# Expert stage of a graph network: blocks of two node tiles and an order for each engine

## What is computed

```
x = x + gnn0(layernorm(x), src, dst, edge_type, ...)   # relational sums over edges
x = x + ffn0(layernorm(x), ...)                        # router, 6 experts, top 2 of them
x = x + gnn1(layernorm(x), edge_attr, edge_weight, ...) # edge attention, then a feed-forward
x = x + ffn1(layernorm(x), ...)                        # router, 8 experts, top 2 of them
```

## Time and profile before

| what | value |
|---|---|
| median of three runs | 1781.44 us |
| the profiled execution, its own time | 1790.08 us |
| its span, first to last instruction | 1788.4 us |
| PE busy, share of the span | 1502.8 us, 84% |
| DVE, ACT, POOL busy | 1012.2, 585.6, 812.5 us |
| mean granted clock of PE | 0.885 |

### The profile page before, as it was taken

One profiled execution on the slowest core, in us unless ns is written; L12 is line 12 of the kernel. 1 busy time (PEld: TensorE's weight loads), 2 busy tenths in 40 slices (PEclk: granted clock), 3 DMA queues, 4 the chain that ended last, 5 costly groups with the idle time before them and its releaser, 6 DMA issues. The chain is left out here.

```text
span 1788.4 us, 22498 instructions
## 1 busy us (share of the span) xinstructions
PE 1502.8 (84%) x6333; PEld 951.4 (53%) x6333; DVE 1012.2 (57%) x2410; ACT 585.6 (33%) x1378; POOL 812.5 (45%) x769
## 2 busy tenths in 40 slices
PE   5999789469598898998736689998989899899996
PEld 3555235135254454456523356676766666676685
DVE  6532343133244453435358778887978787797432
ACT  3211012023132232323112145544445454444431
POOL 1100575757786677100067664745647374550000
PEclk9999659689799899999855689999999999999998
DMA  8356553645665655401188975656556565651100
GB/s 279 139 200 206 151 150 93 187 128 152 164 171 137 185 157 154 132 1 65 65 249 255 272 224 164 195 151 179 167 166 174 161 187 151 190 153 37 31 3 12
DMA packets 191806, 270.00 MB, mean 151 GB/s; under 512 B 28564, under 2 KB 156273, under 8 KB 189105
## 3 DMA queue, kind: packets, MB, share of 16 engines
q1 hardware_dynamic: 147665, 144.74, 26.1%
q0 software_dynamic: 44000, 123.64, 25.1%
HBM read 196.22 MB, written 72.06 MB: 150 GB/s over the span
## 5 line engine op out<-in xcount | busy, mean ns | idle before, releaser
L1853 POOL DMA_INDIRECT att_kv<-table_kv,g_srcI x314 | 366.1, 1166 | 301.2 <-issue 244.4
L1134 POOL DMA_INDIRECT ex_hg<-table_h,z_idx x314 | 322.9, 1028 | 114.6 <-issue 86.6
L1442 PE MATMUL ex_psG<-ex_hg,ex_oh 128*42 128x256 f32 x628 | 128.3, 467 | 91.8 <-issue 78.7
L2377 PE MATMUL att_psR<-att_t,g_mw 128*128 128x256 f32 (+1 forms) x640 | 163.0, 402 | 0.0
L2404 PE MATMUL att_psR<-g_mw,att_h 128*128 128x256 f32 x640 | 159.7, 395 | 1.0 <-ACT att_h L2222 1.0
L1845 POOL DMA_DIRECT2D table_o<-att_part x59 | 53.9, 914 | 208.4 <-DMA table_o<-att_part 134.8
L746 PE MATMUL tab_psH<-e_u,tab_xT 128*128 128x512 f32 x320 | 143.6, 603 | 3.3 <-DVE e_u L527 3.3
L2377 PEld LDWEIGHTS att_psR<-att_t,g_mw 128*128 128x128 f32 x640 | 126.5, 207 | 18.0 <-issue 1.6
L1442 PEld LDWEIGHTS ex_psG<-ex_hg,ex_oh 128*42 128x42 f32 x628 | 42.5, 134 | 173.0 <-issue 134.4
L2404 PEld LDWEIGHTS att_psR<-g_mw,att_h 128*128 128x128 f32 x640 | 122.4, 196 | 22.0 <-ACT att_h L2222 3.9
L1359 ACT ACTIVATE ex_h<-ex_psH,g_cols 128x512 f32<-128x512 f32 (+2 forms) x144 | 86.1, 607 | 139.1 <-PE ex_psH L1457 138.8
(11 more groups left out here) (308 smaller groups left out, 2462.8 us busy)
## 6 DMA issues: line engine op xcount, KB each, us to landing
table_h<-tab_hs SPq DMA_DIRECT2D x20, 1024.0 KB, 4.0
att_eft<-in_eft SPq DMA_DIRECT2D x158, 64.0 KB
ex_db<-table_dst SPq DMA_DIRECT2D x79, 126.0 KB
table_ohT<-ex_ohT SPq DMA_DIRECT2D x79, 126.0 KB
att_ohT<-table_ohT SPq DMA_DIRECT2D x79, 126.0 KB
table_oh<-ex_oh SPq DMA_DIRECT2D x79, 84.0 KB
att_oh<-table_oh SPq DMA_DIRECT2D x79, 84.0 KB
ex_hg<-table_h,z_idx POOLq DMA_INDIRECT x314, 3.8
```

Of the source, the lines that this page charges most:

```text
L1134: nc.gpsimd.indirect_dma_start(hg[:, t % RING0, :], None, d.h[:, :], bass.IndirectOffsetOnAxis(ap=g.idx0[:, t:t + 1], axis=0)).then_inc(go ...
L1442: ins = nc.tensor.matmul(psG[at:at + WG, 0:D], oh[:, i % 3, t % TP, :], hg[:, t % RING0, :], start=(t <= second), stop=(t >= tiles(i)[-1] ...
L1853: nc.gpsimd.indirect_dma_start(kv[:, t % (RINGC * TP), H:H + 2 * D], None, d.kv[:, :], bass.IndirectOffsetOnAxis(ap=g.srcI[:, t:t + 1], ax ...
L2377: ins = nc.tensor.matmul(out[:, c * CB:c * CB + used(b)], g.mw1[:, e, k, c * P:(c + 1) * P], t3[:, k, 0:used(b)], start=(k == 0), stop=(k ...
```

## The change

The blocks become ten of two tiles each. Every engine has a list of its own: `BEGIN0` and `PACE0` place block b on an axis of group numbers (it begins at `BEGIN0[b]`, its pieces lie at `BEGIN0[b] + PACE0[b] * place`), and `GROUP0` places the pieces of each group. `norm` and `post` on DVE are split where they wait for ACT's root; `mix` is split into `gateT` and `bias`; ACT's roots get places of their own. In PSUM a bank of `psH` holds both halves of a layer (2 x 256 columns), `psC` holds two experts in turn, the transposes and the mixed biases use one bank of `psW`. Waits between users of `psW` on PE are found from PE's list (`before`, `taken`). `JOINED_FROM` becomes 50. The weights for q, k and v, and some smaller ones for the next stage, are loaded at groups 8 and 9 rather than 17 and 18; `spots` still begin at 17. `READY_AFTER` becomes 8, 16, 24 and so on to 72, and 78.

By these numbers PE's list begins: groups 0 to 10, `turn` 0, group 11, `hidden` 0, group 12, A0, `logits`, A1, B0, group 13, A2, `gateT`, B1, A3, group 14, `bias`, C0, C1, B2, group 15, ... (expert numbers of block 0). Later, block b's q, k, v products lie among block b + 1's layers A to C.

```diff
-JOINED_FROM = NG // NB + 4
-B0 = (2, 4, 4, 4, 4, 2)
+JOINED_FROM = 50
+B0 = (2,) * 10
+BT0 = max(B0)
+BLK0 = BT0 * P
+BESIDE_FROM = READY_AFTER[0]
...
-ORDER0 = (("hidden", 0, 0), ("A", 0, 0), ("logits", 0, 0), ("A", 0, 1), ("B", 0, 0), ("A", 0, 2), ("B", 0, 1), ("mix", 0, 0), ("C", 0, 0), ("post", -1, 0),
...
+BEGIN0 = (8.50, 18.21, 26.73, 38.53, 45.39, 52.68, 59.85, 67.35, 74.08, 80.63)
+PACE0 = (12.94, 10.92, 15.34, 11.02, 11.48, 10.69, 10.69, 10.36, 10.73, 11.53)
+GROUP0 = {
+    "PE": (("group", 0.127),),
+    "DVE": (("halves", 0.124), ("prepare", 0.781),),
+    "ACT": (("odd", -0.018),),
+    "SP": (("store", 2.347),),
+}
+BLOCK0 = {
+    "PE": (("turn", 0, 0.199), ("hidden", 0, 0.252), ("A", 0, 0.281), ("logits", 0, 0.297), ("A", 1, 0.304), ("B", 0, 0.338),
+           ("A", 2, 0.364), ("gateT", 0, 0.365), ("B", 1, 0.372), ("A", 3, 0.382), ("bias", 0, 0.435), ("C", 0, 0.464), ("C", 1, 0.489),
+           ("B", 2, 0.497), ("A", 4, 0.569), ("B", 3, 0.622), ("C", 2, 0.646), ("A", 5, 0.679), ("C", 3, 0.703), ("B", 4, 0.735),
+           ("B", 5, 0.753), ("C", 4, 0.829), ("q", 2, 0.864), ("C", 5, 0.900), ("turn2", 0, 1.255), ("q", 3, 1.298), ("q", 0, 1.306),
+           ("q", 1, 1.351)),
...
+    "SP": (("kv", 0, 1.675), ("q3", 0, 1.684), ("xu", 0, 2.404)),
+}
+def order0(groups, engine):
+    out = []
     for b in range(NB0):
...
+        out += [(BEGIN0[b] + PACE0[b] * place, what, b, e) for what, e, place in BLOCK0[engine] if what != "q" or e < B0[b]]
+    for i in range(groups):
+        out += [(i + place, what, i, 0) for what, place in GROUP0[engine]]
+    out.sort(key=lambda piece: piece[0])
+    return [piece[1:] for piece in out]
...
-        psC = m.ps("psC", [P, BT, D])
+        psC = m.ps("psC", [P, 2 * BT0, D])
-        mixed = psW[:, :, :].rearrange("p a c -> p (a c)").rearrange("p (t c) -> p t c", t=BT)
+        turns = psW[:, 0, :].rearrange("p (k c) -> p k c", k=DK)
+        mixed = psW[:, 0, :].rearrange("p (t c) -> p t c", t=BT0)
...
-            add_halves(i)
...
+                def normed(b):
+                    t = Tally(s.norm_chain, b, 3, 2)
                     dve.wait_ge(s.std_ready, b + 1)
+                    if b >= 1:
+                        dve.wait_ge(s.turned, b)
...
+                    n = half[what, b, e]
+                    if n >= 3:
+                        pe.wait_ge(s.half_ready, DK * (n - 2))
                     for o in range(DK):
...
+                            ins = nc.tensor.matmul(psH[:, n % 3, o * BLK0:o * BLK0 + w_], w[:, e, k, o * P:(o + 1) * P], x[:, k, 0:w_], start=(k == 0), stop=(k == DK - 1))
+                    ins.then_inc(s.half_made, 1)
...
-                            else:
-                                pe.wait_ge(s.c_used, n - B0[b] + 2)
+                            elif e >= 2:
+                                pe.wait_ge(s.c_used, n - 2 * B0[b] + 2)
```

More of the change, by code:

```diff
@@ L981 @@
[L981 to L989, removed]
-    for b in range(NB0):
[L991 to L997, removed]
@@ new lines @@
+PACE0 = (12.94, 10.92, 15.34, 11.02, 11.48, 10.69, 10.69, 10.36, 10.73, 11.53)
[6 more added lines that the diff above has]
+BLOCK0 = {
[5 rows of a table added]
+    "DVE": (("norm", 0, -0.000), ("normed", 0, 0.078), ("gates", 0, 0.303), ("C", 0, 0.509), ("C", 1, 0.583), ("C", 2, 0.654),
+           ("C", 3, 0.797), ("C", 4, 0.847), ("C", 5, 0.897), ("addx", 0, 1.023), ("post", 0, 1.030), ("post1", 0, 1.066),
+           ("post2", 0, 1.142), ("q", 0, 1.286), ("q", 1, 1.286), ("rest", 0, 1.341), ("q", 3, 1.344), ("low", 0, 1.492),
+           ("biases", 0, 1.528), ("q", 2, 1.605)),
+    "ACT": (("std", 0, 0.017), ("turn", 0, 0.211), ("hidden", 0, 0.239), ("A", 0, 0.281), ("gates", 0, 0.288), ("A", 1, 0.304),
+           ("gateT", 0, 0.309), ("B", 0, 0.338), ("A", 2, 0.364), ("B", 1, 0.372), ("A", 3, 0.382), ("bias", 0, 0.424), ("B", 2, 0.497),
+           ("A", 4, 0.569), ("B", 3, 0.622), ("A", 5, 0.679), ("B", 4, 0.735), ("B", 5, 0.753), ("std1", 0, 1.042), ("std2", 0, 1.095),
+           ("turn2", 0, 1.287), ("high", 0, 1.327), ("mid", 0, 1.377)),
+    "SP": (("kv", 0, 1.675), ("q3", 0, 1.684), ("xu", 0, 2.404)),
+}
@@ L1098, in router, with taken @@
             return v
-        order = blocks_order0() if redo else order0(5.6)
+        orders = {engine: order0(0 if redo else NG, engine) for engine in ("PE", "DVE", "ACT", "SP")}
         half = {}
-        for what, b, e in order:
+        for what, b, e in orders["PE"]:
             if what in ("A", "B"):
-                for o in range(DK):
-                    half[what, b, e, o] = len(half)
+                half[what, b, e] = len(half)
+        assert [v for v in orders["PE"] if v[0] in ("A", "B")] == [v for v in orders["ACT"] if v[0] in ("A", "B")]
+        before, last = {}, None
+        for what, b, e in orders["PE"]:
+            if what in ("turn", "hidden", "logits", "bias", "turn2") or what == "q" and not (b == LAST and e % 2):
+                before[what, b, e], last = last, (what, b, e)
+        def taken(what, b, e):
+            return {"turn": (s.xT_ready, b + 1), "hidden": (s.rhT_ready, b + 1), "logits": (s.gate_chain, b * 20 + 1),
+                    "bias": (s.acc_ready, b + 1), "turn2": (s.x2T_ready, b + 1), "q": (s.qkv_ready, T0[b] + e + 1)}[what]
         def tiles(i):
@@ L1329, in program @@
                         dve.wait_ge(s.ab_ready, 1)
-                    for what, b, e in order:
-                        if what == "group":
-                            group(b)
+                    for what, b, e in orders["DVE"]:
+                        if what == "prepare":
+                            prepare(b)
+                        if what == "halves":
+                            add_halves(b)
                         if what == "norm":
                             norm(b)
-                        if what == "logits":
+                        if what == "normed":
+                            normed(b)
+                        if what == "gates":
                             gates(b)
-                            if b >= 1:
-                                add_x(b - 1)
+                        if what == "addx":
+                            add_x(b)
                         if what == "C":
@@ L1341, in program @@
                         if what == "post":
-                            if b == LAST:
-                                add_x(b)
                             post(b)
+                        if what == "post1":
+                            post_first(b)
+                        if what == "post2":
+                            post_second(b)
                         if what == "q":
                             take_qkv(b, e)
+                        if what == "biases":
+                            add_biases(b)
                         if what == "rest":
-                            add_biases(b)
                             remainder(b)
@@ L1356, in relu @@
                 def relu(what, b, e, o):
-                    n = half[what, b, e, o]
+                    n = half[what, b, e]
                     act.wait_ge(s.half_made, n + 1)
-                    nc.scalar.activation((h1 if what == "A" else h2)[:, e % 2, o, 0:used(b)], psH[:, n % 3, 0:used(b)], ACT.Relu,
+                    nc.scalar.activation((h1 if what == "A" else h2)[:, e % 2, o, 0:used(b)], psH[:, n % 3, o * BLK0:o * BLK0 + used(b)], ACT.Relu,
                                          bias=vec(g, "eb1" if what == "A" else "eb2", 2 * e + o)).then_inc(s.half_ready, 1)
@@ L1366, in program @@
                 def program(_):
-                    for what, b, e in order:
-                        if what == "group":
+                    for what, b, e in orders["ACT"]:
+                        if what == "odd":
                             act.wait_ge(s.summed, b + 1)
@@ L1372, in program @@
                             nc.scalar.copy(odd[:, b % 2, :], psG[P // 2:P // 2 + WG, 0:D]).then_inc(s.odd_ready, 1)
-                        if what == "norm" and b == 0:
+                        if what == "std":
                             root(std, mv, s.var_ready, s.std_ready, b, B0[b])
@@ L1383, in program @@
                                 relu(what, b, e, o)
[L1384 to L1390, removed]
+                        if what == "std1":
+                            root(std2, mv2, s.var2_ready, s.std2_ready, 2 * b, B0[b])
+                        if what == "std2":
+                            root(std2, mv2, s.var2_ready, s.std2_ready, 2 * b + 1, B0[b])
+                        if what == "gates":
                             act.wait_ge(r.shifted, b * 2 + 1)
@@ L1408, in program @@
                             for k in range(DK):
[L1409 removed]
+                                ins = nc.scalar.activation(x2T[:, k, 0:B0[b] * P], turns[:, k, 0:B0[b] * P], ACT.Identity, bias=vec(g, "ln1_b", k),
                                                            scale=vec(g, "ln1_g", k))
```

(13 more changed lines are left out.)

130 lines of the change are left out of this document (61 added, 69 removed).

## The result

The changed kernel takes 1707.92 us in the median of four runs (1704.09 to 1713.35), against 1780.94 us before: a ratio of 0.9587, with a 95% interval of 0.9542 to 0.9632, 73 us less. The forecast was 1751 us with a range of 1712 to 1790: the direction was right, the size was not. The profiled execution took 1709.46 us with a span of 1707.9.

A forecast was written before the change was run, and what follows sets the result against it. PE (TensorE), idle 117.1 of 639 us or at low clock, was the bound. Busy 521.9 + 33 - 15 = 540 plus idle 34 + 22 + 5 + 8 = 69 gave 609, 30 less: 1751 us, range 1712 to 1790.

The forecast's parts named there:

- the idle rate in the sum: PE in the 490 us of blocks outside the tail: idle 6.5% of the time, giving 34 us.
- rival 1: PE fuller than forecast, idling 1% as in 380 to 450 us: 64 us less, 1717 us; chance 0.18.
- Blocks of two tiles fill the holes: PE's group runs before blocks: at most two groups stand together; about 15 us of low-clock work regained.
- Rival 2: Small blocks stall more, waits between engines costing the same beside half the work: 16 us less, 1765 us; chance 0.17.
- SP's stops and slow groups: PE idle behind SP's ten load_sums, 8 us, and where groups at 6.0 us each make it wait, 5 us.
- rival 3: PE waits 9 us for ex_db behind each of seven load_sums: 25 us more, 1806 us; chance 0.10.
- Tail: The last two-tile block's chain keeps its 22.4 us of PE idle time.
- Smaller matmuls: In A and B, 768 instructions of 256 columns replace 384 of 512: 0 us, between -5 and +28.
- the signs: Listed marks of a right or wrong forecast, among them A and B near 220 ns apiece.
- rival 4: Weight loads bound the 256-column stream in A and B at 275 ns apiece: +28 us, 1779 us; chance 0.03.
- The follow products: On PE, 31 more groups carry a product at 1.07 us each: +33 us of work.
- The start: At block 0 DVE waits for sums before group 10's add_halves, 2 or 3 us, done ahead: counted 0.

The follow-up runs named there:

- e4: Changed kernel with normed, post1 and post2 put back right behind norm and post in DVE's list: 1728.79 us, ratio 0.9682 to the kernel before.
- e6: Changed kernel with the one list of the kernel before, translated to the new pieces, for all engines: 1794.39 us, ratio 0.9928 to the kernel before.
- e1: Kernel before with ten blocks of two tiles and nothing else changed: 1782.43 us, ratio 0.9985 to the kernel before.
- e12: Changed kernel with DVE's prepare ahead of halves in groups 0 to 9 and POOL joins from group 19: 1685.76 us, ratio 0.9474.
- e10: Changed kernel with DVE's prepare ahead of halves in groups 0 to 9, products to group 50 kept: 1699.60 us, ratio 0.9547.
- e7: Changed kernel with early prepare in groups 0 to 9 and joins from group 19, on the slower chip: 1710.45 us, ratio 0.9455.
- e8: Changed kernel with early prepare in groups 0 to 9 and products up to group 77, on the slower chip: 1771.04 us, ratio 0.9792.
- e11: Changed kernel with POOL joins from group 19, as in the kernel before, prepare left late: 1703.89 us, ratio 0.9551.
- e9: Changed kernel repeated unaltered as the reference of its set: 1705.89 us, ratio 0.9584 to the kernel before.
- e3: Changed kernel with DVE's prepare ahead of halves in groups 0 to 9, no unaltered kernel beside it: 1697.77 us, ratio 0.9519.
- the second set: Four follow-up runs on one chip, where the kernel before took 1810 us and the unaltered changed kernel 1750.34 us, ratio 0.9690.

## Why the prediction was right or wrong

**The step that failed is the idle rate in the sum**: "the 490 us outside the tail at the rate of the long stretch with blocks and groups well mixed, 9.4 of 144 or 6.5% of the time, give 34". It measured 8.0 us of 477.5, or 1.7%. I had taken the fullest long stretch of the old order as the best that this work allows, without asking what its 9.4 us were. The kernel before, 600 to 744 us, PE's waits; then DVE and PE at the longest of them:

```profile
PE ex_psG L1442 <- issue: 7.0, 3, 5.6
```

```profile
701.13 0.35 DVE L1180 TENSOR_SCALAR ex_ohT<-ex_db,g_qnode 126x512 bf16<-126x512 bf16 x1 [5.79 <-DMA ex_db<-table_dst]
...
701.91 1.94 PE L1442 MATMUL ex_psG<-ex_hg,ex_oh 128*42 128x256 f32 x8 [5.65 <-issue]
```

Of the 9.4 us, 7.0 stand in front of group products, 5.65 of them in a run of groups whose sum lay behind a broadcast on DVE. That is the wait which the change was to remove, so the rate brought it back in, and the terms for slow groups and SP's stops counted it in part a second time. The text also wrote of the split of `norm` and `post` and of `psC` for two experts: "Nothing is counted for either". e4 prices the split alone at some 17 us; e6 prices the own orders, that split among them, at 44 on its chip; e1 shows that without them smaller blocks are worth nothing at all. In the sum the stretch came to 609 us and measured 567, which is nearly the whole miss of 43 us: the 8.5 us behind the stretch are about offset by the median, which lies 1.5 us under the profiled execution where the forecast took 9. The prediction had this as rival 1, 0.18, with 1717 us, 9 above the measurement; its evidence, the full 70 us of 380 to 450, was the better guide.

**Blocks of two tiles fill the holes**: right in the place, wrong in the credit. The big hole is filled in e1 too (16.6 us idle of 80, for 43.4), yet the time is that of before. Rival 2 (small blocks stall more) is true of the one list, where it eats the whole gain, and false of the changed kernel.

**SP's stops and slow groups**, 8 + 5 us: almost nothing of them is seen; no wait of PE for group sums above 1 us is left between 300 and 744 us, and rival 3 with its seven stops of 9 us fell. The stop is 5.2 us at group 24, and the longest wait for `ex_db` 6.6 us.

**Tail**, 22.4 us: 12.9 measured, 9.5 less. I take it that block 8, still running beside block 9, reaches further into it; that was not tried by itself.

**Smaller matmuls**, 0 between -5 and +28: right. 240 ns an instruction against 480 for 512 columns, C at 238 ns without any change in its size. The 240 are above the "near 220" of the signs and under the 250 of rival 4, which fell; PE's busy time was 537.5 us for 540. The 90 us more estimated from the Trainium skill, TensorE: Matmul & The Clock Gate, section Back-to-back issue gap, fell too: for these f32 products the measured time about halves with the columns (at full clock 454 ns an instruction at 512, 216 at 256).

**The follow products**, +33 us: the price about held as PE's busy time (34.7 us for 31 products between e12 and e10, 67.0 for 59 between e7 and e8), but not always as time of the kernel. Between groups 19 and 50 they cost 2 us (e11 against e9) or 13.8 (e12 against e10), since the joins in their place open holes; between 19 and 78 on the other chip they cost 61 us for 59. That they were worth having was not claimed.

**The start**, "done ahead of the block and not twice; 0": wrong, since block 0 begins 17 us later. I followed what is queued behind `norm` on DVE, but not that PE's own group piece ends with transposes that need `prepare`. e3 and e10 confirm the place: block 0 starts 10.4 and 13.7 us sooner with prepare ahead. In e10's median only 6.3 us of that arrive.

## What to carry to other kernels

A mixed stretch that is 93.5% busy is no floor: ask what the rest of it waits for, and whether the change touches that. In this kernel smaller blocks paid only with an order that puts other work behind each wait, on each engine separately; the size by itself traded a big hole for many small ones. When a piece is moved on one engine, look for parts of it that another engine needs within the same step.

## What was not expected of the hardware

The same pair of kernels gave a ratio of 0.9587 and 0.9584 in two measurements and 0.9690 on the chip of the second set, where the kernel before was 28 us slower; the intervals of the single measurements do not cover this. And a follow product costs PE 1.07 us where PE is full, twice the 0.52 us between its start and that of the next matmul (287.74 to 288.26 us in the trace before). The other half is the last tile's two gather matmuls behind it: they take 0.55 us (288.26 to 288.81), while the six in front of it take 1.00 and all eight take 1.00 in a group without it.
